# Two tables of slots are rewritten: where the left-over token block's router, gates and experts stand, and the next image's group statistics

## The reference, cut to what matters

```python
# layer 0, on g = group_norm(x, 32 groups)
q, k, v = Wq@g + bq, Wk@g + bk, Wv@g + bv
attn = softmax(q^T k)                     # 2304 x 2304 for each image
y = sigmoid(relu(mean(g) @ w1.T) @ w2.T)  # squeeze and excite
x = x + gamma * (v @ attn^T) + g * y
# layer 1, on tokens t = x as (2304, 128)
t = t + softmax(ln(t) ln(t)^T) ln(t)      # second attention
u = ln(t)
top2 of softmax(u @ router_w + router_b)  # 8 experts, 2 of them weighted
t = t + sum of the 2 gated (u @ expert_w[e] + expert_b[e])
```

## Time and profile before

| | |
|---|---|
| time, median of 3 runs | 2558.91 us (2558.0 to 2559.78) |
| the profiled execution's own time | 2557.83 us |
| its span | 2556.1 us |
| busy share PE, weight loads | 98%, 90% |
| busy share DVE, ACT, POOL | 83%, 69%, 21% |
| granted TensorE clock | 0.998 |
| chain that ended last | PE 74%, DVE 17%, ACT 5%, issue 3% |

### The profile page before, as it was taken

One profiled execution on the slowest core, in us unless ns is written; L12 is line 12 of the kernel. 1 busy time (PEld: TensorE's weight loads), 2 busy tenths in 40 slices (PEclk: granted clock), 3 DMA queues, 4 the chain that ended last, 5 costly groups with the idle time before them and its releaser, 6 DMA issues.

```text
span 2556.1 us, 45049 instructions
## 1 busy us (share of the span) xinstructions
PE 2501.6 (98%) x14929; PEld 2297.1 (90%) x14929; DVE 2125.3 (83%) x6242; ACT 1774.6 (69%) x3478; POOL 544.6 (21%) x930
## 2 busy tenths in 40 slices
PE   7999999999999999999999999999999999999998
PEld 5889989899898998999989999899998999989997
DVE  6896888878888788887888878888789887898778
ACT  4667766677667776776767767667676677767775
POOL 0010221112220132111321113111141202312134
PEclk9999999999999999999999999999999999999999
DMA  1000000000000000000000000000000000000000
GB/s 68 10 1 1 4 29 1 23 4 7 26 1 23 4 7 26 23 1 4 10 23 23 1 4 10 23 23 1 4 10 23 23 1 4 23 10 4 1 10 13
DMA packets 13621, 32.53 MB, mean 13 GB/s; under 512 B 1616, under 2 KB 8016, under 8 KB 13392
## 3 DMA queue, kind: packets, MB, share of 16 engines
q1 hardware_dynamic: 13392, 29.64, 3.4%
HBM read 20.20 MB, written 9.44 MB: 12 GB/s over the span
## 4 chain that ended last, share of the span: by engine, by line
PE 74%; DVE 17%; ACT 5%; issue 3%; POOL 0%; DMA 0%; ACTq 0%; DVEq 0%; SPq 0%; POOLq 0%
PE ps L1239 22%; PE ps L1241 21%; PE ps L1240 21%; PE ps L1259 9%; DVE pt_lo L1040 5%; DVE row_space L1025 4%; PE ps L1386 1%; ACT row_space L775 1%; DVE pt_lo L1120 1%; ACT pt_hi L786 1%; ACT row_space L827 1%; DVE pt_lo L1125 1%; DVE gn_raw L898 1%; ACT row_space L872 0%; DVE r L1131 0%
## 5 line engine op out<-in xcount | busy, mean ns | idle before, releaser
L786 ACT ACTIVATE pt_hi<-ps 128x384 fp32r<-128x384 f32 x864 | 415.6, 488 | 301.0 <-PE ps L1259 300.7
L1040 DVE TENSOR_TENSOR pt_lo<-ps,pt_hi 128x384 fp32r<-128x384 f32 x864 | 472.6, 551 | 114.2 <-ACT pt_hi L786 112.2
L1025 DVE TENSOR_SCALAR_CACHE_REDUCE row_space<-ps,key_bias 128x512 f32<-128x512 f32 (+1 forms) x720 | 492.0, 689 | 49.0 <-PE ps L1241 48.1
L775 ACT ACTIVATE row_space<-row_space,negmax 128x512 f32<-128x512 f32 (+2 forms) x432 | 402.8, 932 | 86.0 <-DVE negmax L1034 85.2
L1259 PE MATMUL ps<-ident,row_space 128*128 128x128 f32 x2736 | 444.5, 273 | 5.0 <-ACT row_space L775 3.9
L1259 PEld LDWEIGHTS ps<-ident,row_space 128*128 128x128 f32 x2736 | 345.6, 141 | 76.1 <-ACT row_space L775 7.0
L1239 PE MATMUL ps<-pt_hi,v_hi 128*128 128x384 f32 x864 | 352.4, 408 | 17.2 <-DVE pt_lo L1040 14.9
L827 ACT ACTIVATE row_space<-ps,shift 128x768 f32<-128x768 f32 x260 | 234.1, 900 | 137.4 <-PE ps L1241 132.9
L1125 DVE TENSOR_TENSOR pt_lo<-row_space,pt_hi 128x768 fp32r<-128x768 f32 x260 | 251.3, 967 | 91.6 <-ACT pt_hi L836 91.0
L1239 PE MATMUL ps<-pt_hi,tn_hi 128*128 128x384 f32 x864 | 303.5, 351 | 2.2 <-DVE pt_lo L1125 1.1
L1241 PE MATMUL ps<-pt_hi,v_lo 128*128 128x384 f32 x864 | 292.9, 339 | 0.0
(11 more groups left out here) (229 smaller groups left out, 5396.6 us busy)
## 6 DMA issues: line engine op xcount, KB each, us to landing
x_chan<-x SPq DMA_DIRECT2D x24, 384.0 KB, 4.2
y<-acc SPq DMA_DIRECT2D x48, 192.0 KB, 1.8
t_tok<-tokens SPq DMA_DIRECT2D x8, 768.0 KB, 4.3
t_tok<-tokens SPq DMA_DIRECT2D x8, 384.0 KB, 3.1
t_tok<-eb SPq DMA_DIRECT2D x1, 516.0 KB, 5.4
t_tok<-ew SPq DMA_DIRECT2D x1, 516.0 KB, 6.7
row_space<-wqkv SPq DMA_DIRECT2D x1, 192.0 KB, 3.3
se_sb<-se SPq DMA_DIRECT2D x1, 68.0 KB, 4.1
```

The source lines that it names most:

```text
L775: act.activation(part, part, ACT.Exp, bias=negmax[:, r:r + 1], accum_out=dparts[:, n, r, u:u + 1]).then_inc(p_rows_ready, 1)
L786: act.activation(pt_hi[:, slot, :], ring_bank(step)[:, 0:BW], ACT.Copy)\
L1025: dve.tensor_scalar(row_part(n, r, a, w), ring_bank(step)[:, 0:w], key_bias[:, row:row + 1], None, ALU.add, ALU.max, accum_out=mx[:, row % ...
L1040: dve.tensor_tensor(pt_lo[:, slot, :], ring_bank(step)[:, 0:BW], pt_hi[:, slot, :], ALU.subtract).then_inc(pt_lo_ready, 1)
```

## The change

Only the two tables are different. In `EARLIER_BLOCK` the left-over block's router moves from slot (1, 16) to (3, 5), its gates from (2, 1) to (3, 7); the three pairs `expert`, `scaled` move from (3, 6), (3, 9), (3, 12), (3, 13), (4, 4), (4, 9) to (3, 10), (3, 13), (4, 3), (4, 5), (4, 8), (4, 10). In `IMAGE` the first `stat` moves from (4, 17) to (5, 1), and the steps from `gn_dev` to the second `xgnorm` move one or two slots down. No operation is added or removed.

```diff
-EARLIER_BLOCK = {1: {8: [('uln',)], 10: [('uapply',)], 13: [('ut',)], 16: [('router',)]}, 2: {1: [('gates',)]},
-                 3: {6: [('expert', 0)], 9: [('scaled', 0)], 12: [('expert', 1)], 13: [('scaled', 1)]},
-                 4: {4: [('expert', 2)], 9: [('scaled', 2)]}}
+EARLIER_BLOCK = {1: {8: [('uln',)], 10: [('uapply',)], 13: [('ut',)]},
+                 3: {5: [('router',)], 7: [('gates',)], 10: [('expert', 0)], 13: [('scaled', 0)]},
+                 4: {3: [('expert', 1)], 5: [('scaled', 1)], 8: [('expert', 2)], 10: [('scaled', 2)]}}
...
+IMAGE = {(5, 1): [('stat', 0)], (5, 4): [('stat', 1)], (5, 10): [('stat', 2), ('stat', 3)], (5, 12): [('stat', 4)],
```

More of the change, by code:

```diff
@@ L47, in piece_of @@
     return next(u for u, (a, w) in enumerate(EC) if a <= j * TILE < a + w)
-EARLIER_BLOCK = {1: {8: [('uln',)], 10: [('uapply',)], 13: [('ut',)], 16: [('router',)]}, 2: {1: [('gates',)]},
-                 3: {6: [('expert', 0)], 9: [('scaled', 0)], 12: [('expert', 1)], 13: [('scaled', 1)]},
-                 4: {4: [('expert', 2)], 9: [('scaled', 2)]}}
+EARLIER_BLOCK = {1: {8: [('uln',)], 10: [('uapply',)], 13: [('ut',)]},
+                 3: {5: [('router',)], 7: [('gates',)], 10: [('expert', 0)], 13: [('scaled', 0)]},
+                 4: {3: [('expert', 1)], 5: [('scaled', 1)], 8: [('expert', 2)], 10: [('scaled', 2)]}}
 BASE_TILES = {(1, 9): [0], (2, 6): [1], (3, 6): [2], (4, 6): [3], (5, 6): [4], (5, 14): [5]}
-IMAGE = {(4, 17): [('stat', 0)], (5, 4): [('stat', 1)], (5, 10): [('stat', 2), ('stat', 3)], (5, 12): [('stat', 4)], (6,
-         1): [('stat', 5)], (6, 2): [('gn_mean',)], (6, 5): [('gn_dev',)], (6, 8): [('gn_var',)], (6, 10): [('gn_norm',),
-         ('xgnorm', 0)], (6, 12): [('se_in',)], (6, 13): [('xgnorm', 1)], (6, 16): [('se_out',)], (6, 17): [('xgnorm', 2), ('spread',)]}
+IMAGE = {(5, 1): [('stat', 0)], (5, 4): [('stat', 1)], (5, 10): [('stat', 2), ('stat', 3)], (5, 12): [('stat', 4)],
+         (6, 1): [('stat', 5)], (6, 2): [('gn_mean',)], (6, 7): [('gn_dev',)], (6, 9): [('gn_var',)],
+         (6, 11): [('gn_norm',), ('xgnorm', 0)], (6, 13): [('se_in',)], (6, 14): [('xgnorm', 1)], (6, 16): [('se_out',)],
+         (6, 17): [('xgnorm', 2), ('spread',)]}
 L0_SLOTS = {'qproj': 12, 'ot': 4, 'tnt': 15, 'rowsum': 0, 'ln': 5, 'lnapply': 11, 'lnhigh': 15, 'lnlow': 16}
```

## The result

| | before | after |
|---|---|---|
| median of 6 runs each | 2558.29 us (2557.69 to 2559.78) | 2572.22 us (2571.12 to 2573.96) |
| ratio, 95% interval | | 1.0053 (1.0042 to 1.0064) |
| span of the profiled execution | 2556.1 us | 2569.4 us |
| granted TensorE clock | 0.998 | 0.998 |

The changed kernel is 13.9 us slower. The forecast was a sum of +12.0 us and a time of 2570.5 us; the measured 2572.22 lies 1.7 us above it, inside the range of 2563 to 2575. The spans of the two profiled executions differ by 13.3 us.

What follows compares the result with a forecast made beforehand. PE, waiting at hand-overs for a late DVE, was taken as the bound. Parts 1 and 2 (+8.8 us) and part 3 (+3.2) made +12.0 on 2557.83, so 2569.8; 2570.9 in the median's terms, 2570.5 after part 4's small gains; range 2563 to 2575.

Steps and rivals of the forecast that it cites:

- Part 1: Hand-over from block 1 to 2: the router leaves, PE's wait in slot 0 goes; -1.37 us per image, 7 images.
- Part 2, the gates and POOL: Block 3: the gates' first operation runs beside POOL's second `baset` operation and loses 0.68 us; margin 0.18 us.
- Part 2, the chain: Block 3: row maximum of slot 10 delays exponentials, `pt_hi` 14 and `pv` 16; +1.22 us at hand-over 3 to 4.
- Part 2, block 4: `expert` 1 and `scaled` 1 now stand in block 4, where PE is full; +1.40 us per image.
- Part 3: Block 5: the first `stat` displaces what follows, with no slack at `pv` 16; +0.46 us for 7 images.
- Part 4: Block 6: `gn_dev` leaves slot 5, the shorter wait at `pv` 6 is given back; taken as 0, at most -4.8 us.
- gates did not miss POOL: Rival, block 3: the gates start before POOL's second `baset` operation, so POOL waits instead; 2566.1 us, chance 0.20.
- stat wasn't absorbed: Rival, block 5: some slack takes in the first `stat`; +8.8 us, 2567.7 us, chance 0.11.
- pile-up: Rival: four bulky steps in six slots leave a PSUM bank unemptied; 9.6 us more, 2580 us, chance 0.10.
- Mid-block swallows the lateness: Rival, block 3: DVE's and ACT's idle takes up the lateness; 2553.4 us with the first `stat` free too, chance 0.04.

Runs made afterwards that it cites:

- e10: The kernel before with only the router moved, from slot (1, 16) to (1, 17), and the gates, from (2, 1) to (3, 5): 2552.07 us, ratio 0.9972.
- e11: The kernel before with only the router moved, from slot (1, 16) to (1, 17), the gates left in (2, 1): 2557.49 us, ratio 0.9989.
- e8: The changed kernel with the gates in slot (3, 8) instead of (3, 7): 2567.80 us, ratio 1.0034 to the kernel before.
- e3: The kernel before with only the first `stat` moved, from slot (4, 17) to (5, 1): 2563.65 us, ratio 1.0015.
- e12: The kernel before with the router in (1, 17), the gates in (3, 5), and the second `stat` moved from (5, 4) to (5, 17): 2552.71 us.
- e2: The kernel before with the new `IMAGE` alone, `EARLIER_BLOCK` unchanged: 2563.89 us, ratio 1.0014.
- e7: The changed kernel with `expert` 1 put back from (4, 3) to (3, 12) and `scaled` 1 from (4, 5) to (3, 13): 2569.06 us.

## Why the prediction was right

- **Part 1**, -1.37 us per image: measured -1.38. The router's matmuls gave nothing, as taken. But the forecast put all of it down to the router and to slot 0. It needed the gates to leave block 2 as well: with their 0.74 us ahead of the row maximum and 0.12 us of slack, 0.62 us would have come back at the block's end. That is an estimate from e10 against e11; no run moved the router to block 3 and left the gates. That the change moved both was luck for this term.
- **Part 2, the gates and POOL**, a collision worth 0.68 us, with a margin of 0.18: measured 0.69 (0.87 against 0.18) and 0.19, and e8 shows that it is passed on in full. Of the 0.82 us that POOL's operation still ran, the gates lost 0.69, 0.13 less. By the rule of the Trainium skill, page SBUF — State Buffer, section Who interferes with whom, the later one blocks fully, and it would be all of the 0.82. The measurement decides, with the reserve that spans on POOL are rough in this profile.
- **Part 2, the chain**, +1.22 us: measured +1.17. On the way the row maximum came 1.76 us late (said 1.83), counted from the block's start: 1054.57 - 1034.87 = 19.70, against 17.94 before, where it starts at 1049.66. `pt` 14 came 1.40 us late (said 1.57): 25.43 against 24.03. So 0.36 us were swallowed between the two, not 0.26. What came back is at `pv` 16, which started 1.05 us late, not the 1.22 forecast, and then took 0.45 us for its first matmul instead of 0.33. So the sum is right to 0.05 us partly by luck: a start overrated by 0.17 us and a dearer first matmul that the forecast didn't have nearly cancel.
- **Part 2, block 4**, +1.40 us: measured +1.53. The 0.13 us are the term taken as 0, the wait for `pt_lo` 16 at the hand-over 4 to 5, which shows as 0.19 us ahead of the weight load; from the first matmul of `pv` 16 to the block's end it is 0.63 us (1093.25 to 1093.88) against 0.54 before.
- **Part 3**, +0.46 us: measured +0.46, and e3 shows it alone. That block 5 has no slack for a stat *ahead of the row maximum of slot 4* is what holds; e12 shows that behind it there was room for one. The prediction's reason, a row of sums with only 0.19 us of idle, didn't tell these two places apart.
- **Part 4**, 0: measured +0.17 per image, 1.2 us, and -0.47 once in image 7. The 0.4 us that the forecast took off for small gains here went the wrong way. The wait at `pv` 6 did get shorter, from 0.69 to 0.29 us, but an earlier `pv` now waits for 0.21. PE's idle in the block is 0.83 us instead of 0.92, and its busy time 16.50 instead of 16.24. e2 against e3 puts the loss on the steps from `gn_dev` on; which of them makes it no experiment shows, and it stays open.
- **The sum**: +12.0 forecast, +13.3 in the spans. The 1.3 us between them are block 4's 0.13 x 7 and block 6's 0.17 x 7, less 0.47, less the chain's 0.05 x 7.
- **The rivals.** The gates did not miss POOL, and the stat wasn't absorbed. Of the pile-up there was a beginning, PE's 0.38 us for a bank at slot 11 of block 3. The forecast had expected a short wait at `pv` 6 instead. It cost nothing, since the last wait set the end. "Mid-block swallows the lateness" had a true part: DVE's 1.01 us ahead of `pt` 10 went away (counted so in the forecast), and the 0.75 ahead of `pt` 14 didn't count. The forecast gave no reason for the first. It had waited for ACT behind `scaled` 0, which the change takes out of slot 9.

## What to carry to other kernels

Where a reduction on one engine releases a long piece of another, and the first engine then idles for the end of that piece, the idle is slack only for work that stands between the two. Ahead of the reduction the same work moves the whole chain: in block 2 it was 9.53 us from the row maximum to the end in each of the four variants with no extra work behind it, and 0.74 us of gates ahead of it cost 0.75. Look first what the idle really waits for: in block 3 it hung on PE's matmuls, and there the gates were free on either side. Before a step is moved, look whether it passes another one on each of its engines, what its own inputs queue behind, and which operation of another engine it will run beside; and count a lateness from the block's start to the chain's head, never from the last idle gap alone.

## What the runs showed that I had not expected

- Leaving a wait makes PE's group longer, too: the first matmul of `pv` 16 took 0.44 or 0.45 us behind an idle stretch (0.45 in the changed kernel, 0.44 in e7 and e8) and 0.33 without one, so a wait costs some 0.11 us more than its idle time here. The ends of matmuls are modelled in the profile, but the starts bear it out: 1.05 us of late start became 1.17 us of block 3. Why the group is longer isn't shown.
- A version beats both kernels: e10, router in (1, 17) behind `pt` 17, gates in (3, 5), at 2552.07 us, 0.28% below the kernel before (0.17 to 0.39%).
